# A fused attention and MLP layer on one core: the loop over bands written out, orders of three engines and two PSUM banks changed, maxima subtracted by half tiles

## The reference

```
h1  = n1_w * arcsinh(x) + n1_b
q, k, v = split(h1 @ qkv_w + qkv_b)             # 8 heads of 32
for each position: scores = q . k over its 3 x 3 neighbours (windows clipped at the image edge)
attn = softmax(scores);  o = attn @ v
h   = x + o @ proj_w + proj_b
h2  = n2_w * arcsinh(h) + n2_b
out = h + gelu(h2 @ mlp_w1 + mlp_b1) @ mlp_w2 + mlp_b2     # 256 -> 512 -> 256
```

## Time and profile before

| | |
|---|---|
| median of 3 runs | 4895.31 us (4894.92 to 4899.79) |
| the profiled execution | 4905.26 us |
| its span | 4903.5 us |
| busy PE / POOL / DVE / ACT | 89% / 82% / 76% / 68% of the span |
| mean granted TensorE clock | 0.975 |
| DMA | 600.50 MB, 16 engines 46% busy |

### The profile page before, as it was taken

How to read it: one execution, slowest core, us unless ns; L and a number is a source line. 1 busy time by engine, 2 the same in 40 slices (tenths; PEclk the granted TensorE clock), 3 DMA queues, 4 the chain that set the end, 5 groups by cost and what they waited for, 6 DMA issues and landing times.

```text
span 4903.5 us, 149526 instructions
## 1 busy us (share of the span) xinstructions
PE 4361.5 (89%) x53320; PEld 3118.8 (64%) x53320; DVE 3743.8 (76%) x7717; ACT 3345.0 (68%) x4865; POOL 4044.6 (82%) x5498
## 2 busy tenths in 40 slices
PE   3899899999999989999999989989999998999997
PEld 2666666666666666666666666666666666666665
DVE  4777777877777777778777778777777777787784
ACT  2676677777677666767767667676776767677674
POOL 1788888888888888888888888888888888888885
PEclk9999999999999999999999999999999999999998
DMA  3454444444444444444445444444544444454441
GB/s 79 127 130 121 124 127 127 125 127 125 123 130 126 122 125 126 126 124 130 125 122 130 121 127 126 125 124 123 131 126 122 129 123 124 122 131 125 121 124 54
DMA packets 593557, 600.50 MB, mean 122 GB/s; under 512 B 76558, under 2 KB 540560, under 8 KB 590352
## 3 DMA queue, kind: packets, MB, share of 16 engines
q1 hardware_dynamic: 592912, 591.32, 46.2%
HBM read 197.69 MB, written 135.40 MB: 68 GB/s over the span
## 4 chain that ended last, share of the span: by engine, by line
POOL 47%; issue 32%; PE 15%; ACT 3%; POOLq 1%; DVE 1%; SPq 1%; DMA 0%; ACTq 0%; DVEq 0%
PE ps L384 15%; POOL p_lo L1055 9%; POOL b_lo L1074 8%; POOL g_lo L1084 7%; POOL g_hi L1082 6%; POOL k_win L1102 5%; POOL gate L1049 5%; POOL b_hi L1072 3%; POOL k_win L1112 2%; ACT p_hi L991 2%; POOL k_win L1121 1%; ACT L1000 1%; POOLq L1052 0%; ACT prob L990 0%; POOL a_lo L1064 0%
## 5 line engine op out<-in xcount | busy, mean ns | idle before, releaser
L1055 POOL TENSOR_TENSOR p_lo<-prob,p_hi 100x512 f16<-100x512 f32 x1024 | 1347.4, 1330 | 272.7 <-ACT p_hi L991 272.7
L990 ACT ACTIVATE prob<-ps 100x512 f32<-100x512 f32 x1024 | 615.7, 601 | 960.8 <-PE ps L384 959.7
L818 DVE TENSOR_REDUCE ps<-ps 128x8 f32<-128x800 f32 x512 | 510.5, 997 | 280.4 <-PE ps L384 280.4
L1049 POOL TENSOR_TENSOR gate<-gate_in 1x1 f32<-1x1 f32 x894 | 285.9, 320 | 492.2 <-DVE ln_u L744 434.3
L849 DVE TENSOR_TENSOR o_norm<-ps,recip 64x128 f32<-64x128 f32 x2048 | 591.4, 289 | 52.1
L1084 POOL TENSOR_TENSOR g_lo<-g,g_hi 128x512 f16<-128x512 f32 x512 | 591.9, 1156 | 41.0
L991 ACT ACTIVATE p_hi<-ps 100x512 f16<-100x512 f32 x1024 | 617.7, 603 | 0.0
L384 PEld LDWEIGHTS ps<-v_win,p_hi 100*128 100x128 f16 x8192 | 483.8, 98 | 181.5 <-issue 16.0
L384 PE MATMUL ps<-w_hi,g_hi 128*128 128x256 f16 x2048 | 560.8, 274 | 0.0
L384 PE MATMUL ps<-w_lo,g_hi 128*128 128x256 f16 x2048 | 560.7, 274 | 0.0
L384 PE MATMUL ps<-w_hi,g_lo 128*128 128x256 f16 x2048 | 560.6, 274 | 0.0
(11 more groups left out here) (105 smaller groups left out, 12397.6 us busy)
## 6 DMA issues: line engine op xcount, KB each, us to landing
keys<-k_win SPq DMA_DIRECT2D x1536, 100.0 KB, 2.2
v_win<-v_rows SPq DMA_DIRECT2D x1024, 101.6 KB
queries<-q_nat SPq DMA_DIRECT2D x1536, 64.0 KB
v_rows<-v_nat SPq DMA_DIRECT2D x256, 260.0 KB, 4.5
xin<-in_x_dram SPq DMA_DIRECT2D x128, 512.0 KB, 4.0
out_dram<-y SPq DMA_DIRECT2D x256, 256.0 KB, 2.7
queries<-in_query_mask_dram SPq DMA_DIRECT2D x128, 160.0 KB
keys<-in_mlp_w_dram SPq DMA_DIRECT2D x2, 512.0 KB, 6.2
```

The lines of the kernel that those rows point to most:

```text
L818: v.tensor_reduce(maxima_of_pair(), ps[:, B_S:B_S + 2, 0:PAIRS * NK].rearrange("p n (a k) -> p n a k", k=NK), AX.X, ALU.max).then_inc(max3 ...
L990: act.activation(prob[b][0:NK], ps[0:NK, B_ST + b, :], ACT.Exp, scale=INV * INV).then_inc(prob_ready, 1)
L1049: pool.tensor_tensor(gate[:, n:n + 1], gate_in[:], gate_in[:], ALU.add)
L1055: pool.tensor_tensor(p_lo[b][0:NK], prob[b][0:NK], p_hi[b][0:NK], ALU.subtract).then_inc(p_lo_ready, 1)
```

## The change

The loop is written out: all 133 steps are straight code, and with it every register in a wait or an address becomes a constant. key_max is cut to 64 rows per tile: the maxima of a slot's first tile stand in rows 0 to 63, those of the second in rows 64 to 127, each subtraction is contracted over its 64 rows, and the two tiles' matmuls alternate. X_BANK becomes [1, 0] and V_BANK [2, 1], and the waits that go with them change. PE, DVE, ACT and POOL get other orders in some slots. POOL's gates go.

```diff
-X_BANK = [1, 2]
-V_BANK = [0, 1]
+X_BANK = [1, 0]
+V_BANK = [2, 1]
 # run
-            for t in range(-3, XT):
-                step(t, t % XT)
-            with eng.Fori(0, BANDS // XT - 2) as i:
-                for n in range(XT):
-                    step(i * XT + (XT + n), n)
-            for t in range(BANDS - XT, BANDS + 2):
+            for t in range(-3, BANDS + 2):
                 step(t, t % XT)
 # x_transposes, g == 1
-                    pe.wait_ge(q_lo_ready, signals(t - 1, G, 1))
+                    pe.wait_ge(q_lo_ready, signals(t - 1, G, 2))
 # v_product, n == 0
-                    pe.wait_ge(q_lo_ready, signals(t, G, 2))
+                    pe.wait_ge(q_lo_ready, signals(t, G, 1))
 # mlp_out: n == 0 waits v_lo_ready(t + 4, first), n == 1 waits xT_ready(t + 5, second)
-            def subtract_max(t, c):
-                k = c // 2
-                if c % 2 == 0:
-                    pe.wait_ge(maxrow_ready, signals(t, SLOTS, k + 1))
+            def subtract_max(t, k):
+                pe.wait_ge(maxrow_ready, signals(t, SLOTS, k + 1))
                 for p in range(PAIRS):
-                    s = mm(ps[:, B_ST + c % 2, p * P:(p + 1) * P], key_max[:, (c % 2) * PAIRS + p, :], max_row[k % 2][:],
-                           stop=True)
-                s.then_inc(pe_st, 1)
+                    for n in range(2):
+                        r = slice(MROW * n, MROW * n + MROW)
+                        s = mm(ps[:, B_ST + n, p * P:(p + 1) * P], key_max[r, p, :], max_row[k % 2][r, :], stop=True)
+                        if p == PAIRS - 1:
+                            s.then_inc(pe_st, 1)
 # PE step, slot 1
                         x_transposes(t + 3, 0)
+                    if k == 1 and pre:
+                        v_product(t + 2, 0)
+                    if k == 1 and fill:
                         x_transposes(t + 3, 1)
                     if k == 1 and pre:
-                        v_product(t + 2, 0)
                         v_product(t + 2, 1)
 # DVE maxima_to_rows
-                v.tensor_copy(max_row[k % 2][r, :], ps[r, B_S, MAXT_COLS].bitcast(BF16)).then_inc(maxrow_ready, 1)
+                v.tensor_copy(max_row[k % 2][:], ps[:, B_S, MAXT_COLS].bitcast(BF16)).then_inc(maxrow_ready, 1)
```

More of the change, by code:

```diff
@@ L40 @@
 INV = 1.0 / WS
-M0 = 32
+MROW = P // 2
 MASK0 = 3 * HD
@@ L51 @@
 N_LOADS = 14 + 2 * PAIRS
-N_ZERO = 12
+N_ZERO = 11
 V_BV, V_ALL = 1, 23
@@ L228, in maxima_of_pair, with maxima_columns @@
         def maxima_of_pair():
-            return ps[:, B_S, MAX_COLS]
+            return ps[:, B_S, MAX_COLS].rearrange("p (n a) -> p n a", n=2)
+        def maxima_columns(b, lo):
+            return maxima[b][:].rearrange("p (n r) -> p n r", n=2)[:, :, lo * PAIRS:(lo + 1) * PAIRS]
         def turned(o, half):
@@ L538, in mlp_out @@
                     pe.wait_ge(g_lo_ready, signals(t, MT, MT))
[L539 to L542, removed]
+                    if has(t + 4):
+                        pe.wait_ge(v_lo_ready, signals(t + 4, 2, 1))
                     else:
                         pe.wait_ge(gelu_ready, signals(t, MT, 4))
+                elif has(t + 5):
+                    pe.wait_ge(xT_ready, signals(t + 5, G, 2))
                 elif has(t + 4):
-                    pe.wait_ge(v_lo_ready, signals(t + 4, 2, 1))
+                    pe.wait_ge(q_lo_ready, signals(t + 4, G, 2))
                 elif has(t + 1):
@@ L828, in maximum_low @@
                 b = k % 2
[L829 to L830 removed]
+                v.tensor_tensor(maxima_columns(b, 1), maxima_of_pair(), maxima_columns(b, 0), ALU.subtract).then_inc(max_ready, 1)
             def maxima_to_rows(t, k):
                 v.wait_ge(pe_max, signals(t, SLOTS, k + 1))
[L834 to L835 removed]
+                v.tensor_copy(max_row[k % 2][:], ps[:, B_S, MAXT_COLS].bitcast(BF16)).then_inc(maxrow_ready, 1)
             def sum_reciprocal(t, c):
@@ L867, in step @@
                         k_low(t + 2, 0)
-                    if k == 1 and post:
-                        magnitude2(t - 1, old)
                     if k == 1 and pre:
                         q_low(t + 2, par, 0)
+                    if k == 2 and post:
+                        sign2(t - 1, old)
                     if k == 2 and fill:
                         magnitude1(t + 3, (u + 3) % XT)
-                    if k == 2 and post:
-                        sign2(t - 1, old)
                     if k == 3 and att:
                         o_low(t, par, 0)
+                    if k == 3 and fill:
+                        sign1(t + 3, (u + 3) % XT)
                     if att:
@@ L903, in step @@
                     if k == 2 and fin:
-                        result(t - 2, 1)
-                    if k == 3 and fill:
-                        sign1(t + 3, (u + 3) % XT)
+                        result(t - 2, 0)
                     if att:
@@ L910, in step @@
                         normalise(t, 2 * k + 1)
+                    if k == 0 and post:
+                        magnitude2(t - 1, old)
                     if k == 1 and pre:
                         v_low(t + 2, 1)
+                    if k == 2 and fin:
+                        result(t - 2, 1)
             run(v, step)
@@ L1007, in step @@
                         probabilities(t, 2 * k)
+                    if k == 0 and post:
+                        o_high(t - 1, old, 1)
                     if k == 2 and post:
@@ L1013, in step @@
                         probabilities(t, 2 * k + 1)
-                    if k == 0 and post:
-                        o_high(t - 1, old, 1)
                     if k == 0 and pre:
@@ L1045, in _ @@
             pool.wait_ge(zeroed, N_ZERO)
-            def pass_waits(n):
-                pool.tensor_tensor(gate[:, n:n + 1], gate_in[:], gate_in[:], ALU.add)
             def p_low(t, c):
@@ L1129, in step @@
                         p_low(t, 2 * k)
-                    if k == 2 and pre:
-                        windows_main(t + 2, par, 1)
-                    if att:
                         p_low(t, 2 * k + 1)
@@ L1143, in step @@
                         b_parts(t - 1)
+                    if k == 2 and pre:
+                        windows_main(t + 2, par, 1)
                     if k == 3 and fill:
```

34 lines of the change are left out of this document (11 added, 23 removed).

## The result

The changed kernel takes 4490.98 us (median of 4 runs, 4489.97 to 4493.34) against 4895.11 before: ratio 0.9173, 95% interval 0.9157 to 0.9189. The prediction was 4460 (4340 to 4620). The profiled execution has a span of 4491.5.

A forecast was written before the change was run, and what follows sets the result against it. It took TensorE, delayed by late POOL work, and POOL, blocked by DVE, as near-equal bounds. Span 4903.5 - 136 (jumps) - 300 (bands 36.04 to 33.6) - 4 = 4463, hence 4455, say 4460 us; range 4340 to 4620.

The forecast's parts named there:

- Jumps, -136: Loop written out: all 29 jumps go at 4.7 us each, straight code costs nothing; -136 us.
- rival D: Straight code is fetched too slowly, TensorE stalls at each band's code; about 5050 us, chance 0.04.
- The waits of the new band: TensorE's waits left per band: 0.2 for q_lo, 0.2 for b_lo, 0.5 for p_low(6), 0.45 for a_lo.
- POOL's account, 27.2 + 4.7 + 1.7: POOL per band: 27.2 us work and gaps, 4.7 blocked by DVE, 1.7 waiting for exponentials and sign1; 33.6.
- the prediction's 0.9: POOL's loss in us when an operation meets a two-input DVE operation, against the full 1.2 by the port rule.
- rival B: POOL and DVE's exclusion binds harder or the halves do not overlap; 34.3 to 35.2 a band, 4540 to 4650, chance 0.15.
- Subtraction, -0.5 us a band: Subtraction by half tiles on TensorE: halves overlap, 0.41 instead of 0.54 us per slot, four slots a band.
- TensorE's 32.7 - 0.5: TensorE's band without gaps, 32.7 us, less 0.5 for the half-tile subtraction: 32.2.
- Gates, -1.0 of POOL work: Seven gates removed on POOL, 0.13 to 0.18 us each: 1.0 us less POOL work per band.
- The sum: Bands of 33.6 instead of 36.04 us, no jumps, 4 less at the ends: span 4463, time say 4460.
- A's 33.0: Upper end of the rival that TensorE is packed and its three waits vanish: 32.3 to 33.0 a band, chance 0.15.
- C's new waits: Rival: waits for gathers, y before mlp_in(1) or p_low(6) replace the old; 35.2 to 36 a band, chance 0.06.

The follow-up runs named there:

- e1: The kernel before with the loop written out and nothing else; 4765.5 us, ratio 0.9738.
- e4: The changed kernel with the last windows_main back between the two p_low of slot 2 on POOL; 4514.7 us.
- e10: The changed kernel with the copies of k's high part into the windows moved from POOL to ACT, behind k_high; 4490.4 us.
- e3: The changed kernel with the old subtraction of the maxima over all 128 rows, one tile after the other; 4490.5 us.
- e7: The changed kernel with POOL's last windows_main split: first copy between the two p_low of slot 2, second behind b_parts; 4473.6 us.
- e11: As e10, with the low part's window copies also moved up to slot 1 on POOL, behind g_parts; 4449.9 us, ratio 0.9092.
- e12: The changed kernel with the subtraction's matmuls left out, so work is missing; 4435.5 us.
- e9: The changed kernel with the same 64-row matmuls, the first tile's four and then the second's four, not alternating; 4488.9 us.

## Why the prediction was right

Point by point, by its own steps.

- **Jumps, -136.** -129 by e1's medians. The 3.57 us of issue and the lower clock behind it were read rightly, straight code costs nothing, and rival D is gone: 133 steps in a row without such a stall.
- **The waits of the new band: 0.2 (q), 0.2 (b), 0.5 (p_lo in slot 3), 0.5 (a_lo), 1.4 in all.** Measured 0.3 + 0.2 (xT), 0.22, 0.58 and 0.33: 1.6. Following the orders by hand gave place and size of each, the new one before p_low(6) too, which windows_main behind b_parts causes. e4 shows that the place was worth 24 us all the same.
- **POOL's account, 27.2 + 4.7 + 1.7.** The blocked time is 4.6. A meeting costs the rest of the DVE operation less 0.13 to 0.15 us, so the prediction's 0.9 (1099.59 + 1.21 - 0.13 - 1099.77) was the part that was left, and no sign against the port's being held to the end: the full 1.2, which it set against the 0.9 and used for rival B, is only the bound for two operations that start together. The waits for exponentials are 0.30, 0.50 and 0.76 before three of the p_lo in the band, 1.56. The terms held. What I concluded from them, that POOL leaves no room since its work fills the band, did not: e10 took 2.3 us a band off POOL's busy time and nothing changed. What e3, e7, e10, e11 and e12 fit is a chain through POOL, ACT, DVE and a piece of TensorE, in which POOL's part is the stretch from p_low(5) to a_parts.
- **Subtraction, -0.5 us a band.** The duration was right (0.43, forecast 0.41 per slot, both halves beside each other, as the Trainium skill has it for row groups in TensorE: Matmul & The Clock Gate, the part on packing small matmuls, with starts about 4 ns apart; the trace agrees, 3 to 4 ns). Its worth was wrong: it is 0 (e3). The prediction did name a delay of the first tile, 0.1, but put it down to the seventh matmul, where it is the change of shape, and called ACT "not waiting there". It waits there for 0.56 us (1081.09 above). This step failed: TensorE's 32.7 - 0.5 was taken as part of the sum, in a band where TensorE was not the bound. As a count of TensorE's work it is right (33.86 less 1.6 of waits is 32.2); but without the half tiles the waits are shorter and the band is the same (33.84).
- **Gates, -1.0 of POOL work.** Worth 0.48 a band, 67 us. They lie partly in POOL's waits.
- **The sum.** 33.6 a band was predicted and 33.86 measured; 123 x 0.26 = 32 us, less 4 more than forecast at the two ends, is the 28 between the forecast span of 4463 and the measured 4491.5. That the times themselves lie 31 apart has in it the rounding from 4455 up to 4460. Of the 0.26, 0.2 is in the longer waits; I can't place the rest. The account that gave the 33.6 was the following of the orders by hand, wait by wait. That POOL's account came to 33.6 too is luck in part: its terms are right, but it is no reason for the period, as e10 shows.
- **The rivals.** 33.86 is above A's 33.0 and below B's 34.3. Of C's new waits only the one for p_low(6) came, 0.58; for the gathers TensorE waited once in the whole execution, 1.8 us.

Taken singly, the undone parts cost 127 + 67 + 30 + 24 + 0 = 248 us of the 274 between e1 and the changed kernel. The other 26 must be in the moves that were not undone alone (magnitude2, sign2, o_high, the results) and in what the parts do together.

## What to carry to other kernels

When no engine is full, ask of each edit on which wait it ends: 0.11 us a slot taken from the busiest engine was worth nothing, and 1.4 us of copies a band moved out of the way of one short operation behind them on POOL was worth 41 us (e10 to e11). A faster form of a group that finishes its first member later is no gain for who waits for the first. And a hardware loop costs what its jump stalls the busiest engine, here 3.7 to 4.5 us a turn.

## What the runs showed of the hardware

- Matmuls of 64 rows in the two row halves run beside each other, each pair 55 to 67 ns behind the last from start to start, also when the program has all of one half first; the second half's then start ahead of earlier ones (e9, 13 ns behind their partners).
- Each change of tile shape on TensorE costs about 0.1 us here: 1063.16 + 0.47 to 1063.73 into the half rows, and again out of them (1063.73 + 4 x 0.056 to 1064.06).
- A DVE sum or sign (two SBUF inputs) or magnitude (one), each of 128x1024, and a POOL operation exclude each other, in both directions: POOL loses 0.5 us to a magnitude and 0.7 to 1.0 to a sum or sign, and DVE up to 0.8 (1084.91: 1.65 instead of 0.85; sign1 in e11: 1.98 instead of 1.23). POOL's operation gets going 0.13 to 0.15 us before the DVE record ends.
